# A 2-D Fourier mixing block on one core: the spectrum laid out image by image, the first transform in twelve groups of wider products

## The chip, the cores and the metric

The kernel runs on one NeuronCore of a Trainium2 chip. The metric is the device time of one execution in microseconds (us). The engines have their own instruction streams and meet by semaphores: TensorE (PE in the profile, its weight loads PEld), VectorE (DVE), ScalarE (ACT), GpSimd (POOL) and SyncE (SP), which only issues transfers here.

## What is computed

The input x is 4 images of 64 x 64 pixels with 16 channels, all float32. Two residual blocks follow each other. The change lies in the first half of the first one:

```python
h  = layernorm(x) @ w_te + b_te                  # 16 -> 32 channels
F  = fft2(h, axes=(1, 2))                        # over y and x
fr = concatenate([real(F), imag(F)])             # 64 channels
fc = gelu(fr @ w_fc + b_fc)                      # first channel mix, 64 -> 64
re, im = fc[..., :32], fc[..., 32:]
sp = real(ifft2(re + 1j * im))
x1 = x + sp @ w_tp + b_tp                        # second channel mix, 32 -> 16
h2 = layernorm(x1) @ w_fe + b_fe
x2 = x1 + gelu(depthwise3x3(h2) + b_dw) @ w_fp + b_fp
```

The second block (a 3x3 convolution to 192 channels, products of 8 x 8 Fourier patches, a layernorm, a gate and a projection) follows; the change leaves it alone.

## The kernel before, in words

Since the transform is linear, the kernel transforms the 16 normalised channels and not the 32 widened ones; `w_te` is folded into the weights of the first mix (`wmix1`), and the second mix (`wmix2`, 32 -> 16 channels) is done in the frequency domain too. Of the 64 frequencies u along y only U = 33 are computed.

**Load.** SP issues x in three pieces (group 0 in two halves, then group 1), `weights`, `more`, `w_qkv` and `norm2`; ScalarE issues `first` (tile `kf`, L600) and `taps`. A group g is two images; a plane is [128 rows (2 images x 64 y), 64 x] per channel. VectorE centres and normalises (L825 to L841), ScalarE squares and takes deviations (L612, L617); the result goes by channel into `sq` (`planes(g)`).

**First transform** (over y, TensorE, L1091 to L1106). Eight groups j of four channels; for each channel two products with the plane as the stationary operand, and `f1c` (cosines) or `f1s` (minus sines) as the moving one, 66 columns each (2 images x 33 u). They write partitions 0 to 63 and 64 to 127 of a PSUM bank. VectorE evacuates the even groups (L875), ScalarE the odd ones (L652 and L672), both by `f1_evac` (L325) into `f1`, which lies in the tile `spec`, channels innermost, so that the copy writes with a stride of 64 floats. `conv_weights` (L1076, which folds `w_qkv` for the second block and waits for its transfer) stands between groups 3 and 4. Five banks are used, so groups 5 to 7 wait for copies of earlier ones.

**Second transform** (over x, L1119 to L1130). For each u two products of 64 columns, with `dre` and `dim`, whose stationary operand is `f1[:, u]` (4 images x 16 channels = 64 columns). They give the real part on partitions 0 to 63 and the imaginary part on 64 to 127, rows ordered (part, image, channel). VectorE copies the banks into `sp` (L881), in five spans of 512 (the last of 64) frequencies.

**First mix** (`mix1`, L1156). For each span and each of the four images 64 output features are wanted twice over (128 columns, two sign patterns `s`), from the image's 16 real and 16 imaginary channels. These lie in different halves of the partitions. So a product takes 32 rows (the real or imaginary channels of two images, of which `wmix1` zeroes those of the other image), and each image takes two products that accumulate in one bank: a round of four (`again` false), a semaphore wait (`m1_half`), and a second round of four. The order of images is `QUADS`, the banks are `MIX_BANKS`. ScalarE applies Gelu to each bank (L685) into `gl`, which holds two spans.

**Second mix and column turn.** `mix2` (L1146) multiplies with `wmix2`, VectorE copies the result into `hc` (L886); `ht_step` (L1132) turns eight u with 64-column products, VectorE copies to `ht` (L889, L891). The order on TensorE, written out by hand at L1172 to L1183, is for span n: mix1(n), mix2(n-1), ht_step(n-2). Then comes the inverse transform (L1193, L1203).

**Beside it.** `wmix1` is made by ScalarE in eight copies (L664 to L667) from the product of `w_te` and `w_fc` in bank 7 (L1067), scaled by `smix` (GpSimd, L538); `hb` carries the bias to frequency zero (L669, L671; `mix_bias`, L1109). Behind group 7 ScalarE copies the folded conv weights (L676, L677) and loads the Gelu table; SP waits for that copy to issue eight loads of `wc` and eight of `wc9` (L448, L451), then the row of ones (L454, which waits for the last mix2); GpSimd waits for it to split the weights (L553 to L556) and then adds `b_tp` to x (L563).

## Time and profile before

| | us |
|---|---|
| runs (3) | 228.74, 226.67, 226.41; median 226.67 |
| profiled execution | 227.11 |
| its span, first to last instruction | 225.3 |
| TensorE busy in the span | 208.6 (93%) |
| VectorE, ScalarE, GpSimd busy | 156.2, 129.4, 77.2 |
| mean granted clock of TensorE | 0.997 of full speed |

Times in the rows are counted from the start of the span. A timeline row is: start, length, engine, line, operation, output and input tile, shapes, how many instructions are merged, and in brackets how long the engine had been idle and who released it. A row of a group is: line, engine, operation, tiles, shapes, count, then busy us, mean ns of one, then idle time before. A float32 matmul of the kernel appears as two instructions, so a count x8 is four products. Matmuls overlap; the length of a single one (some 220 ns for 64 columns) is mostly latency, and a merged row or a piece of the chain tells the rate. "DMA a<-b" is a transfer.

### The profile page before, as it was taken

The page shows a single profiled execution, that of the slowest core. Times are in us where ns is not written, and L with a number is a line of the kernel's source. Part 1 is how long each engine was busy: PE and PEld are TensorE (multiplying, and loading weights), DVE is VectorE, ACT ScalarE, POOL GpSimd, SP SyncE. Part 2 cuts the span into 40 slices and gives each one's busy share as a digit, 9 for nine tenths or more (in the row PEclk, how much of TensorE's full clock was granted, in tenths as well). Part 3 has the DMA queues.
Part 4 walks back from the last instruction along what each step waited for, and adds up shares of the span by engine and source line. Part 5 has one row for each costly group of instructions (what it writes and reads, how often), then busy time and mean ns, then how long its engine had stood idle before and what let it go on. Part 6 is the DMA issues. An engine that isn't in the chain of part 4 may idle for free.

```text
span 225.3 us, 4554 instructions
## 1 busy us (share of the span) xinstructions
PE 208.6 (93%) x1742; PEld 130.2 (58%) x1742; DVE 156.2 (69%) x286; ACT 129.4 (57%) x271; POOL 77.2 (34%) x70
## 2 busy tenths in 40 slices
PE   7969999898799999988899999999999999999973
PEld 3349624666357547864657565666657575665461
DVE  3995313539963991957886777897768986697693
ACT  3358176514384762754856767566665757565532
POOL 1553700000340000000166544663456435667800
PEclk9999999999999999999999999999999999999998
DMA  6940000000000039699999799999100000000002
GB/s 214 326 100 8 17 11 0 22 3 3 4 0 0 0 121 227 165 189 180 206 193 246 188 211 206 217 215 225 51 0 23 3 23 1 3 0 23 1 3 70
DMA packets 26006, 20.83 MB, mean 92 GB/s; under 512 B 5130, under 2 KB 24602, under 8 KB 25882
## 3 DMA queue, kind: packets, MB, share of 16 engines
q1 hardware_dynamic: 25355, 20.04, 42.4%
q10 hardware_dynamic: 629, 0.50, 0.8%
q8 instruction: 14, 0.23, 0.5%
q14 instruction: 8, 0.07, 0.1%
HBM read 16.36 MB, written 4.02 MB: 90 GB/s over the span
## 4 chain that ended last, share of the span: by engine, by line
PE 65%; DVE 14%; DMA 10%; ACT 4%; issue 3%; SPq 1%; ACTq 1%; DVEq 0%
PE psum L1293 22%; PE psum L1306 11%; PE psum L1325 6%; DMA wq<-w_qkv 5%; PE psum L1164 5%; PE psum L1237 4%; DMA parts<-tr 3%; PE psum L1343 2%; PE psum L1142 2%; PE psum L1152 2%; PE psum L1125 2%; PE psum L1369 2%; DVE tr L850 2%; DMA arena<-parts 2%; PE psum L1245 2%
## 5 line engine op out<-in xcount | busy, mean ns | idle before, releaser
L1293 PEld LDWEIGHTS psum<-wc,tile 128*128 128x128 f32 (+1 forms) x376 | 50.7, 160 | 25.7 <-issue 15.5
L1293 PE MATMUL psum<-wc,tile 128*128 128x192 f32 (+1 forms) x376 | 59.8, 309 | 3.1 <-DVE tile L386 1.4
L581 POOL TENSOR_TENSOR zp<-zp,ln 128x512 f32<-128x512 f32 x14 | 17.9, 1278 | 84.4 <-DVE zp L996 84.4
L1237 PE MATMUL psum<-arena,wdw 102*128 102x512 f32 x48 | 22.2, 597 | 1.3 <-ACT arena L341 1.3
L765 ACT ACTIVATE zp<-zp 128x512 f32<-128x512 f32 x15 | 9.5, 630 | 18.0 <-DVE zp L985 18.0
L969 DVE TENSOR_TENSOR arena<-psum,arena 128x1024 f32<-128x1024 f32 x15 | 18.3, 1219 | 1.8 <-ACT arena L754 1.8
L979 DVE TENSOR_REDUCE stat<-psum 128x8 f32<-128x512 f32 x16 | 11.0, 690 | 11.9 <-PE psum L1325 10.7
L582 POOL TENSOR_TENSOR zp<-zp,ln 128x512 f32<-128x512 f32 x14 | 18.2, 1298 | 1.1
L386 DVE COPY tile<-arena 128x256 f32<-128x256 f32 x64 | 15.3, 298 | 2.6 <-DMA arena<-parts 1.8
L612 ACT ACTIVATE sq<-xc 128x512 f32<-128x512 f32 x12 | 7.6, 637 | 16.4 <-DVE xc L829 16.4
L990 DVE TENSOR_REDUCE stat<-zp 128x8 f32<-128x512 f32 x15 | 10.3, 686 | 9.7 <-ACT zp L765 9.7
L386 ACT COPY tile<-arena 128x128 f32<-128x128 f32 x60 | 15.9, 318 | 1.4 <-DMA arena<-parts 1.4
L747 ACT COPY spec<-psum 128x768 f32<-128x768 f32 x16 | 12.6, 789 | 7.2 <-PE psum L1293 7.2
L1325 PE MATMUL psum<-arena,km 128*64 128x512 f32 x60 | 16.2, 617 | 0.4 <-DVE tr L855 0.4
L1306 PE MATMUL psum<-spec,km 64*128 64x512 f32 x64 | 15.9, 615 | 0.0
L685 ACT ACTIVATE arena<-psum,wt 128x512 f32<-128x512 f32 (+1 forms) x20 | 10.6, 612 | 9.0 <-PE psum L1164 9.0
L754 ACT COPY arena<-psum 128x1024 f32<-128x1024 f32 x15 | 14.9, 995 | 0.3 <-PE psum L1306 0.3
L1237 PEld LDWEIGHTS psum<-arena,wdw 102*128 102x128 f32 x48 | 8.5, 189 | 10.0 <-issue 8.6
L985 DVE SCALAR_TENSOR_TENSOR zp<-stat,psum 128x512 f32<-128x512 f32 x16 | 11.0, 688 | 1.8 <-DVE stat L979 0.5
L741 ACT COPY arena<-psum 128x512 f32<-128x512 f32 x16 | 9.5, 591 | 4.4 <-PE psum L1357 3.5
L886 DVE COPY spec<-psum 128x512 f32<-128x512 f32 (+1 forms) x5 | 3.0, 597 | 12.6 <-PE psum L1152 12.6
L996 DVE TENSOR_TENSOR zp<-zp,stat 128x512 f32<-128x512 f32 x16 | 11.1, 692 | 0.5
(138 smaller groups left out, 362.5 us busy)
## 6 DMA issues: line engine op xcount, KB each, us to landing
arena<-padded SPq DMA_DIRECT2D x12, 393.0 KB, 9.3
arena<-parts SPq DMA_DIRECT2D x12, 196.5 KB, 8.9
arena<-padded SPq DMA_DIRECT2D x6, 262.0 KB, 9.3
arena<-padded SPq DMA_DIRECT2D x8, 195.0 KB, 4.3
wq<-w_qkv SPq DMA_DIRECT2D x1, 1296.0 KB, 12.3
padded<-tr SPq DMA_DIRECT2D x4, 264.0 KB, 2.6
parts<-tr SPq DMA_DIRECT2D x9, 115.5 KB
out<-xt SPq DMA_DIRECT2D x8, 128.0 KB, 1.7
```

The lines of the kernel that those rows point to most:

```text
L386: o = copy(dst[:, n % 2, 2 * h:2 * h + 2].rearrange("p a (q x y) -> p (a q) x y", q=2, x=8), a)
L581: pool_link(pool.tensor_tensor(y, y, along(0), ALU.mult))
L582: pool_link(pool.tensor_tensor(y, y, along(1), ALU.add))
L747: act.copy(qkv[n // 2 % 4][:, n % 2].rearrange("p (a t) c -> p a (t c)", a=2), psum[:, 512 * conv_base(n):512 * conv_base(n) + 1024].rearr ...
L754: act.copy(kh, psum[:, 2048:3072]).then_inc(k_ev, 1)
L969: dve.tensor_tensor(pr, psum[:, 1024:2048], kh, ALU.mult).then_inc(prod, 1)
L996: dve.tensor_tensor(y, y, per_group(s[:, 3, :]), ALU.mult).then_inc(signal, 1)
L1164: last = mm(mix_bank(n, turn)[:, 0:w], wmix1[rows, b].rearrange("p s n -> p (s n)"), sp[rows, spans(n)], start=(n > 0 and not again), stop ...
L1237: last = mm(bank[4 + t4][:, :], wdw[:, dy].rearrange("p x h -> p (x h)"), uw[0:KW, 4 * t4:4 * t4 + 4, 2 * g:2 * g + 2, dy:dy + S], start=( ...
L1293: last = mm(bank[conv_base(n) + a][:, HID * h:HID * h + HID], stationary[:, n % 2, 2 * h + a, :], moving, start=first and h == 0, stop=not ...
L1306: last = mm(bank[2 + 2 * part + q][:, :], const(name)[rows], src, start=True, stop=True)
L1325: last = mm(o_bank(i)[64 * q:64 * q + 64, :], const("inv4"), pr[:, 512 * q:512 * q + 512], start=True, stop=True)
```

## The change

The moving matrices of the first transform become `f1a` and `f1b`, which each give real and imaginary part of the y transform, 132 columns. `f1a` (partitions 0 to 63) gives (cos, -sin), `f1b` (64 to 127) gives (-sin, -cos). `f1` becomes twice as large, [u, image, part, channel], and moves into the arena; the copy writes with a stride of 128 floats. A bank holds three channels of 132 columns, so there are twelve groups (four of three and two of two channels per pair of images), five for VectorE and seven for ScalarE. The second transform now uses `dre` alone and takes one image pair per product; the rows of `sp` come out as (image, part, channel), so an image's 32 values are one block of 32 partitions. `mix1` is then one round of four 32-row products, without accumulation and without `m1_half`; `wmix1` needs two copies instead of eight. On ScalarE the copies of the first transform now all stand behind `wmix1` and `hb`; on TensorE conv_weights stands between groups 5 and 6, behind group 5's wait for the copy of group 0.

```diff
-FIRST, NFIRST = columns(("f1c", 2 * U), ("f1s", 2 * U), ("mask", 2 * NB), ("sign", 1))
-MORE, NMORE = columns(("dre", S), ("dim", S), ("selre", S), ...
+FIRST, NFIRST = columns(("f1a", 4 * U), ("f1b", 4 * U), ("mask", 2), ("sign", 1))
+MORE, NMORE = columns(("dre", S), ("selre", S), ...
...
-QUADS = (0, 2, 1, 3)
 MIX_BANKS = (7, 3, 4, 0, 1, 5, 6, 7, 3, 4, 0, 1, 5, 7, 3, 4, 0, 1, 5, 7)
+F1_GROUPS = [(g, slice(c, min(c + n, C))) for g in range(G2) for c, n in ((0, 3), (3, 3), (6, 3), (9, 3), (12, 2), (14, 2))]
+F1_VECTOR, F1_SCALAR = (4, 5, 6, 8, 10), (0, 1, 2, 3, 7, 9, 11)
...
-    put("f1c", np.einsum("ab,yu->aybu", eye2, np.cos(th)).reshape(P, 2 * U))
-    put("f1s", np.einsum("ab,yu->aybu", eye2, -np.sin(th)).reshape(P, 2 * U))
+    put("f1a", np.einsum("ab,ryu->aybru", eye2, [np.cos(th), -np.sin(th)]).reshape(P, 4 * U))
+    put("f1b", np.einsum("ab,ryu->aybru", eye2, [-np.sin(th), -np.cos(th)]).reshape(P, 4 * U))
...
-        f1 = spec[:, 0:UV].rearrange("p (u b c) -> p u b c", u=U, b=NB)
+        f1 = arena[:, 12416:12416 + 2 * UV].rearrange("p (u b r c) -> p u b r c", u=U, b=NB, r=2)
...
-        wmix1 = sb("wmix1", [P, NB, 2, 2 * H0])
+        wmix1 = sb("wmix1", [P, 2, 2 * H0])
...
-            return bank[(0, 1, 2, 3, 4, 0, 1, 2)[j]]
+            return bank[j % 5 if j < 6 else (j - 5) % 5]
...
-            src = f1_bank(j)[:, 0:4 * 2 * U].rearrange("p (c b u) -> p c b u", c=4, b=2)
-            return copy(f1[:, :, 2 * g:2 * g + 2, 4 * c4:4 * c4 + 4].rearrange("p u b c -> p c b u"), src)
+            src = f1_bank(j)[:, 0:4 * U * n].rearrange("p (c b u) -> p c b u", c=n, b=4)
+            return copy(f1[:, :, 2 * g:2 * g + 2, :, cs].rearrange("p u b r c -> p c (b r) u"), src)
...
             square(0, 0)
             deviation(0, 0)
-            square(0, 1)
-            deviation(0, 1)
-            for j in (1, 3):
-                act.wait_ge(f1_mm, j + 1)
-                f1_evac(act.copy, j).then_inc(f1_act, 1)
-
             act.wait_ge(ld_w, 16)
...
             act.activation(wmix2[:, :], const("tp"), ACT.Copy, scale=const("sign")).then_inc(mix_ready, 1)
+            square(0, 1)
+            deviation(0, 1)
...
-            for b in range(NB):
-                for s in range(2):
-                    act.activation(wmix1[:, b, s, :], bank[7][:, 0:2 * H0], ACT.Copy,
-                                   scale=smix[:, NB * s + b:NB * s + b + 1]).then_inc(mix_ready, 1)
-
+            for s in range(2):
+                act.activation(wmix1[:, s, :], bank[7][:, 0:2 * H0], ACT.Copy, scale=smix[:, s:s + 1]).then_inc(mix_ready, 1)
             act.activation(hb[:, 0:1], bank[7][0:H0, 64:65], ACT.Identity, bias=vec("b_te", H0)).then_inc(act_chain, 1)
-            act.wait_ge(act_chain, 1)
-            act.activation(hb[:, 1:2], hb[:, 0:1], ACT.Copy, scale=float(S * S)).then_inc(mix_ready, 1)
-            for j in (5, 7):
+            for j in F1_SCALAR:
                 act.wait_ge(f1_mm, j + 1)
                 f1_evac(act.copy, j).then_inc(f1_act, 1)
+                if j == 0:
+                    act.wait_ge(act_chain, 1)
+                    act.activation(hb[:, 1:2], hb[:, 0:1], ACT.Copy, scale=float(S * S)).then_inc(mix_ready, 1)
...
-            for j in range(0, 8, 2):
+            for j in F1_VECTOR:
                 dve.wait_ge(f1_mm, j + 1)
                 f1_evac(dve.tensor_copy, j).then_inc(f1_dve, 1)
...
-            for r in range(2):
-                mm(bank[7][64 * r:64 * r + 64, 0:2 * H0], const("teT", H0), fc[:, r, :], start=True, stop=True)
+            te_T = const("teT", H0)
+            for b in range(NB):
+                for r in range(2):
+                    mm(bank[7][H0 * b:H0 * b + H0, 0:2 * H0], te_T[:, H0 * r:H0 * r + H0], fc[:, r, :], start=(r == 0), stop=(r == 1))
...
-            for j in range(8):
-                g, c4 = divmod(j, 4)
-                if j == 4:
+            for j, (g, cs) in enumerate(F1_GROUPS):
+                if j == 5:
+                    pe.wait_ge(f1_act, 1)
+                if j == 6:
                     conv_weights()
-                if j == 5:
-                    pe.wait_ge(f1_dve, 1)
-                if j == 6:
-                    pe.wait_ge(f1_act, 1)
-                if j == 7:
-                    pe.wait_ge(f1_dve, 2)
+                    pe.wait_ge(f1_act, 2)
+                if j in (7, 8):
+                    pe.wait_ge(f1_act, j - 4)
+                if j >= 9:
+                    pe.wait_ge(f1_dve, j - 8)
                 pe.wait_ge(z_done, half_no(0, g, 1))
-                for c in range(4):
-                    for r, name in enumerate(("f1c", "f1s")):
-                        last = mm(f1_bank(j)[64 * r:64 * r + 64, 2 * U * c:2 * U * (c + 1)], planes(g)[:, 4 * c4 + c, :], const(name),
-                                  start=True, stop=True)
+                for c in range(cs.start, cs.stop):
+                    for r, name in enumerate(("f1a", "f1b")):
+                        at = 4 * U * (c - cs.start)
+                        last = mm(f1_bank(j)[64 * r:64 * r + 64, at:at + 4 * U], planes(g)[:, c, :], const(name), start=True, stop=True)
                 last.then_inc(f1_mm, 1)
...
-            pe.wait_ge(f1_act, 2)
-            pe.wait_ge(f1_dve, 3)
-            for turn in range(3):
-                mix_bias(turn)
+            mix_bias(0)
+            pe.wait_ge(f1_dve, 4)
+            mix_bias(1)
+            pe.wait_ge(f1_act, 6)
+            mix_bias(2)
             pe.wait_ge(ld_more, 16)
-            pe.wait_ge(f1_act, 4)
-            pe.wait_ge(f1_dve, 4)
+            pe.wait_ge(f1_act, 7)
+            pe.wait_ge(f1_dve, 5)
...
                 for u in range(8 * n, min(8 * n + 8, U)):
-                    for r, name in enumerate(("dre", "dim")):
-                        last = mm(f2_bank(n)[64 * r:64 * r + 64, S * (u % 8):S * (u % 8) + S],
-                                  f1[:, u].rearrange("p b c -> p (b c)"), const(name), start=True, stop=True)
+                    for g in range(G2):
+                        last = mm(f2_bank(n)[64 * g:64 * g + 64, S * (u % 8):S * (u % 8) + S],
+                                  f1[:, u, 2 * g:2 * g + 2].rearrange("p b r c -> p (b r c)"), const("dre"), start=True, stop=True)
...
-                for turn, b in enumerate(QUADS):
-                    r = turn // 2 if not again else 1 - turn // 2
-                    rows = slice(64 * r + 32 * (b // 2), 64 * r + 32 * (b // 2) + 32)
-                    at = NB * n + turn
-                    if MIX_BANKS[at] in MIX_BANKS[:at] and not again:
+                for b in range(NB):
+                    rows = slice(H0 * b, H0 * b + H0)
+                    at = NB * n + b
+                    if MIX_BANKS[at] in MIX_BANKS[:at]:
                         pe.wait_ge(gelu1, max(i for i in range(at) if MIX_BANKS[i] == MIX_BANKS[at]) + 1)
-                    last = mm(mix_bank(n, turn)[:, 0:w], wmix1[rows, b].rearrange("p s n -> p (s n)"), sp[rows, spans(n)],
-                              start=(n > 0 and not again), stop=again, skip_group_check=(n == 0))
-                    if again:
-                        last.then_inc(m1_mm, 1)
-                if not again:
-                    last.then_inc(m1_half, 1)
+                    mm(mix_bank(n, b)[:, 0:w], wmix1[rows].rearrange("p s n -> p (s n)"), sp[rows, spans(n)],
+                       start=(n > 0), stop=True, skip_group_check=(n == 0)).then_inc(m1_mm, 1)
...
                 pe.wait_ge(f2_ev, 5 if n == 1 else n + 1)
-                mix1(n, False)
-                pe.wait_ge(m1_half, n + 1)
-                mix1(n, True)
+                mix1(n)
```

## Rows read from the trace of the kernel before

**Rows 1.** page of the profile: granted clock in 40 slices, chain by engine

```profile
PEclk9999999999999999999999999999999999999998
...
PE 65%; DVE 14%; DMA 10%; ACT 4%; issue 3%; SPq 1%; ACTq 1%; DVEq 0%
```

**Rows 2.** chain of waits, first 48 us: start, us, what

```profile
3.07 12.32 DMA wq<-w_qkv
...
15.44 1.52 PE psum L1081 x16
...
17.57 2.02 PE psum L1104 x64
...
20.34 3.94 PE psum L1125 x128
...
24.86 1.11 PE psum L1164 x8
...
26.01 3.03 PE psum L1164 x16
...
45.23 2.72 PE psum L1193 x118
```

**Rows 3.** timeline, 10 to 20 us: start, us, engine, line, operation

```profile
12.02 2.09 PE L1104 MATMUL psum<-kf,sq 128*64 128x66 f32 x64 [0.95 <-DVE sq L841]
...
14.53 0.32 ACT L617 ACTIVATE st<-st,eps 128x32 f32<-128x32 f32 x1 [0.47 <-DVE st L835]
...
16.33 1.66 ACT L666 ACTIVATE wmix<-psum,smix 128x64 f32<-128x64 f32 x8
...
17.50 1.95 PEld L1104 LDWEIGHTS psum<-kf,sq 128*64 128x64 f32 x64 [0.30 <-DVE sq L841]
...
17.89 0.24 ACT L669 ACTIVATE hb<-psum,wt 32x1 f32<-32x1 f32 x1
...
19.63 0.60 ACT L325 COPY spec<-psum 128x264 f32<-128x264 f32 x1 [0.32 <-PE psum L1104]
```

**Rows 4.** groups of instructions by line and shape, 0 to 60 us

```profile
L841 DVE TENSOR_TENSOR sq<-xc,st 128x512 f32<-128x512 f32 x4 | 4.3, 1068 | 0.1
...
L881 DVE COPY arena<-psum 128x512 f32<-128x512 f32 x4 | 2.8, 692 | 2.5 <-PE psum L1125 2.5
...
L325 ACT COPY spec<-psum 128x264 f32<-128x264 f32 x4 | 2.3, 628 | 0.6 <-PE psum L1104 0.6
L325 DVE COPY spec<-psum 128x264 f32<-128x264 f32 x4 | 2.3, 614 | 0.5 <-PE psum L1104 0.3
...
L677 ACT COPY x<-psum 128x384 f32<-128x384 f32 x1 | 0.5, 457 | 0.0
```

**Rows 5.** DMA issues, 0 to 20 us

```profile
kf<-first ACTq DMA_DIRECT2D x1, 70.5 KB, 3.3
```

**Rows 6.** timeline, 27 to 43 us, the channel mixes

```profile
27.17 2.42 ACT L685 ACTIVATE arena<-psum,wt 128x512 f32<-128x512 f32 x4 [4.91 <-PE psum L1164]
27.91 0.29 PEld L1164 LDWEIGHTS psum<-arena,wmix 32*128 32x128 f32 x2 [0.73 <-ACT arena L685]
...
30.16 1.07 PE L1152 MATMUL psum<-arena,wmix 128*32 128x512 f32 x8
...
31.16 2.37 PE L1164 MATMUL psum<-arena,wmix 32*128 32x512 f32 x16
...
34.45 1.15 PE L1142 MATMUL psum<-km,spec 128*64 128x64 f32 x32
...
39.91 0.99 PE L1164 MATMUL psum<-arena,wmix 32*128 32x64 f32 x16
...
42.90 0.32 PE L1152 MATMUL psum<-arena,wmix 128*32 128x64 f32 x8
```

**Rows 7.** timeline, work issued behind the copies of the conv weights

```profile
22.39 4.40 POOL L563 TENSOR_TENSOR xt<-xt,wt 128x512 f32<-128x512 f32 x4
...
26.32 6.03 SPq L451 DMA_DIRECT2D wc<-w9s  x8
```

More of the change, by code:

```diff
@@ L85, in constants @@
     put("dre", np.concatenate([co, si]))
-    put("dim", np.concatenate([-si, co]))
-    mask = np.zeros((2, NB, C, 2, NB))
-    for b in range(NB):
-        mask[:, b, :, 0, b] = 1
-        mask[0, b, :, 1, b] = 1
-        mask[1, b, :, 1, b] = -1
-    put("mask", mask.reshape(P, 2 * NB))
+    mask = np.ones((NB, 2, C, 2))
+    mask[:, 1, :, 1] = -1
+    put("mask", mask.reshape(P, 2))
     sign = np.ones((P, 1))
@@ L149, in put @@
         w[row:row + a.shape[0], lo:lo + a.shape[1]] = a
-    for b in range(NB):
-        put("teT", i["L0_conv_w_te"].T, at=C * b)
+    for r in range(2):
+        put("teT", i["L0_conv_w_te"].T, at=3 * C * r)
     put("te", i["L0_conv_w_te"])
@@ L236, in two_blocks @@
         ui9_pairs = arena[:, 3 * UW:4 * UW].rearrange("p (i x t y) -> p i x t y", i=2, x=8, t=8)
-        smix = sb("smix", [P, 2 * NB])
-        wmix1 = sb("wmix1", [P, NB, 2, 2 * H0])
+        smix = sb("smix", [P, 2])
+        wmix1 = sb("wmix1", [P, 2, 2 * H0])
         hb = sb("hb", [H0, 2])
@@ L680, in _ @@
                 w = spans(n).stop - spans(n).start
-                for turn, b in enumerate(QUADS):
-                    act.wait_ge(m1_mm, NB * n + turn + 1)
+                for b in range(NB):
+                    act.wait_ge(m1_mm, NB * n + b + 1)
                     if n >= 2:
                         act.wait_ge(m2_mm, n - 1)
-                    act.activation(gl[:, n % 2, b, 0:w], mix_bank(n, turn)[:, 0:w], ACT.Gelu, bias=vec("b_fc")).then_inc(gelu1, 1)
+                    act.activation(gl[:, n % 2, b, 0:w], mix_bank(n, b)[:, 0:w], ACT.Gelu, bias=vec("b_fc")).then_inc(gelu1, 1)
             load_table(ACT.Sqrt)
@@ L1153, in mix2, with mix1 @@
                 last.then_inc(m2_mm, 1)
-            def mix1(n, again):
+            def mix1(n):
                 w = spans(n).stop - spans(n).start
-                for turn, b in enumerate(QUADS):
-                    r = turn // 2 if not again else 1 - turn // 2
-                    rows = slice(64 * r + 32 * (b // 2), 64 * r + 32 * (b // 2) + 32)
-                    at = NB * n + turn
-                    if MIX_BANKS[at] in MIX_BANKS[:at] and not again:
-                        pe.wait_ge(gelu1, max(i for i in range(at) if MIX_BANKS[i] == MIX_BANKS[at]) + 1)
-                    last = mm(mix_bank(n, turn)[:, 0:w], wmix1[rows, b].rearrange("p s n -> p (s n)"), sp[rows, spans(n)],
-                              start=(n > 0 and not again), stop=again, skip_group_check=(n == 0))
-                    if again:
-                        last.then_inc(m1_mm, 1)
-                if not again:
-                    last.then_inc(m1_half, 1)
+                for b in range(NB):
+                    rows = slice(H0 * b, H0 * b + H0)
+                    at = NB * n + b
+                    if MIX_BANKS[at] in MIX_BANKS[:at]:
+                        pe.wait_ge(gelu1, max(i for i in range(at) if MIX_BANKS[i] == MIX_BANKS[at]) + 1)
+                    mm(mix_bank(n, b)[:, 0:w], wmix1[rows].rearrange("p s n -> p (s n)"), sp[rows, spans(n)],
+                       start=(n > 0), stop=True, skip_group_check=(n == 0)).then_inc(m1_mm, 1)
             pe.wait_ge(m1_bias, NB)
```

15 lines of the change are left out of this document (8 added, 7 removed).

## The prediction

> **What bounds the kernel now.** I read the page first: the chain that ended last is 65% TensorE and 14% VectorE, and the granted clock is at its upper level (2.4 GHz) in all but the last of 40 slices [rows 1]. So in the stage that the change touches, the question is what TensorE does or waits for. The chain of waits in order of time answers it [rows 2]: the `w_qkv` transfer lands at 15.40; conv weights (L1081, L1084) run 15.44 to 17.57; the second group's first transform 2.02 us; then an evacuation and the mix bias until 20.34; the second transform to 24.86; then the two channel mixes and the column turn (`ht_step`) until the inverse transform starts at 45.23. From 15.4 to 45.2 this is TensorE nearly throughout. The timeline shows who works beside it [rows 3, 6], the groups by shape give prices [rows 4].
>
> All times below are of the profiled execution: 227.11 us, which is a span of 225.3 and 1.8 around it. It lies 0.44 above the median 226.67 of the three runs; I take that off at the end.
>
> **Part 1, the mix: one round instead of two.** Start to start, L1152 at 30.16, L1164 at 31.16 and L1142 at 34.45 [rows 6]: 3.29 from the start of two rounds of mix1 to that of the column turn, of which mix2 takes 1.00 (30.16 to 31.16), so the two rounds take 2.29, and one with its gap 1.15; the first round of all has 1.11 and then 0.04 until the next at 26.01 [rows 2]. The short span's two rounds take 0.99 with their tail [rows 6], say 0.49 each. The change drops four of the long and one of the short: 4 x 1.18 is at most 4.7, plus 0.45: about 5.1 us of TensorE.
>
> Not all of it reaches the end, because ScalarE's Gelu takes 2.42 us for a span of four [rows 6], more than the 1.15 of a round. I walk the stage, with mix1(0) starting at t = 0, a product ready 1.15 after its round starts (26.01 to 27.17), a Gelu 0.605 (2.42 / 4), mix2 1.00 and ht 1.08 (1.15 with its tail, less the 0.07 by which mix2's 1.07 exceeds 1.00), and 0.06 for a semaphore:
> - Gelu span 0: 1.15 to 3.57. mix1(1) starts at 1.11, but its fourth product needs bank 7, as now (TensorE waits 0.73 for that Gelu [rows 6]); it starts at 1.89 and ends at 3.0.
> - Gelu 1: 3.57 to 5.99. mix2(0) must wait for Gelu 0: 3.63 to 4.67, after an idle 0.6. mix1(2) to 5.78. Gelu 2: 5.99 to 8.41.
> - mix2(1) waits for Gelu 1: 6.05 to 7.09 (idle 0.27). ht(0) to 8.17, mix1(3) to 9.28; Gelu 3: 9.32 to 11.74.
> - mix2(2) to 10.28, ht(1) to 11.36, mix1(4) to 11.81, mix2(3) to 12.85, ht(2) to 13.93, mix2(4) to 14.18, ht(3) to 15.29; two VectorE copies and a semaphore, as now, and L1193 starts at 16.2.
>
> Now it is 45.23 - 24.86 = 20.37. So 4.2 us are gained, and 0.9 of the 5.1 goes into waits for Gelu. The Trainium skill warns of just this (TensorEngine Tiling (Array Packing), PSUM Bottleneck): once tiling has made TensorE faster, the evacuation of PSUM may be the limit. If Gelus alone set the stage, the last would end about 1.0 earlier than in my walk, so the rule gives no worse time; here it takes 0.9 of the gain.
>
> **Part 2, the first transform: twice the columns.** Per channel there are still two products (four instructions), in two column groups that overlap. Now: 2.02 / 16 = 126 ns a channel with 66 columns [rows 2]. What do 66 more cost? L1152 with 64 and with 512 columns takes 0.32 and 1.07 us for two instructions per column group [rows 6]: 0.75 / (2 x 448) = 0.84 ns per column and instruction, so 2 x 66 x 0.84 = 110 ns. A channel becomes 236 ns, 16 of them 3.78 us instead of 2.02. Bounds: 220 ns (nothing but columns) and 252 (twice 126), 3.52 and 4.03 us. Gaining below 220 is the first rival. I take 236, from the row of the same kind of instruction.
>
> The Trainium skill (TensorEngine Tiling (Array Packing), Instruction Overhead) gives each matmul some 60 cycles beside its columns. By that a channel would rise by (132 + 60) / (66 + 60), to 192 ns; no row here has 132 columns.
>
> **Part 3, who evacuates and in what order.** `f1` doubles, so copies are of 396 or 264 elements. Strided 264 cost VectorE 0.61, strided 512 (L841) about 1.05 [rows 4]: 1.7 ns an element, so 396 cost 0.84. ScalarE: 264 cost 0.605 [rows 3, 4]; with 0.2 fixed, 396 cost 0.81. Bounds for ScalarE: 0.46, the plain copy of 384 (L677), and 1.21, two of today's. I take 0.81, nearest to the row with the same kind of write. The stride between written elements doubles (256 to 512 bytes); VectorE's plain and strided rows (0.69 and 1.07 for 512) tell only that striding costs, not how it grows.
>
> ScalarE no longer copies at 14.75 but first makes `wmix1` (2 instead of 8) and `hb`: the deviations end at 14.85 [rows 3], 2 at 1.66 / 8 and hb 0.24 bring it to 15.48, the copy of group 0 ends at 16.29. Only then may TensorE begin group 5 (bank 0 again), and conv_weights stands behind group 5:
> - Group 5 (2 channels): 16.35 to 16.82. Conv weights, 17.57 - 15.44 = 2.13 [rows 2], to 18.95. Today they started with the landing; this moved wait costs 1.4.
> - Second group: 18.95 + 3.78 = 22.73. Its bank waits are covered: ScalarE's copies 1, 2, 3 end at 17.3, 18.1 and 18.9 (with hb's 0.2 between), TensorE needs them at 18.95, 19.7 and 20.4; VectorE is free after the normalise that released 17.50 [rows 3] and copies 4 and 5 by 18.5, group 6 by 20.6, needed at 22.3.
> - Group 11: copied 22.77 to 23.38, against 19.63 to 20.23 [rows 3]. The mix bias fits beside it. The second transform starts at 23.46 instead of 20.34: 3.12 us later. Its work is unchanged (same instructions, same 64 columns).
> The weight copies of ScalarE (L676, L677) come 3.1 later, and behind them SP's loads of `wc` and POOL's additions: these ended at 32.35 and 26.79 [rows 7], now at 35.5 and 29.9; both are needed only behind the inverse transform that starts at 44 [rows 2], so this costs nothing. SP's next load, the row of ones, waits behind them for mix2(4), at about 42: 6 us are left; without that cover the depthwise stage would wait for it. The Gelu table is loaded in time too.
>
> **Part 4, the loads.** `first` grows by 126 columns (63 KB), `more` shrinks by 64 (32 KB). `kf` is issued together with the first half of x and took 3.3 us for 70.5 KB [rows 5]; in that stretch the kernel's queues share the engines. The start at 3.85 may move by 0 to 0.2; everything in part 3 hangs on it, so I take 0.1. The eight tiny products for `wmix1` run where TensorE idles 0.95 before 12.02 [rows 3]: nothing.
>
> **Sum.** +3.12 + 0.1 - 4.17 (20.37 - 16.2) = -0.95, and the inverse transform starts at 44.3. From there the chain is bound to the shifted work, so I pass all of it on: 227.11 - 0.95 = 226.16, and on the scale of the median 225.7 us.
>
> **Rivals.**
> - A, wider products are cheaper than I say. Weight loads are busy 1.95 of the 2.09 us of a 16-channel stretch [rows 3], so these and not the columns may set 126 ns today. If a channel cost 192, the second group is 0.70 and group 5 0.09 shorter: 224.9 (on the median's scale). Against: the 0.84 ns per column, which makes 220 from columns alone. This is what the skill's 60 cycles would give.
> - B, slower than before: ScalarE's copies set the pace. At 1.5 us for 396 elements, group 0 is out at 16.98, group 5 and the conv weights end at 19.6, and copies 1, 2, 3, 7, 9 run back to back: 18.7, 20.2, 21.7, 23.2, 24.7; then group 11's 1.0: the second transform starts at 25.8, 5.4 later instead of 3.1: 228.0. It decides above about 1.2 us a copy: there the copies are back to back and the gain of 4.2 is used up (transform at 24.3, +4.0, and 0.1 of part 4). For: 1.21 is today's price per element without any fixed part, and the stride doubles. Against: VectorE's rows show a fixed part.
> - C, the gain is not passed on: a later stage with its own pace (a DMA, 10% of the chain [rows 1]) absorbs the 0.95: 226.7. For: such transfers stand in the chain. Against: behind the mixes they are loads of what the kernel itself has just stored, so they shift too.
> - D, the clock falls in the new idle of 1.1 us before group 5. At half the clock, conv weights, second group and half of the second transform take 8 us longer: 234. Against: today TensorE idles 1.33 us just there (14.11 to 15.44) and the clock stays up [rows 1 to 3].
>
> **Chances.** Forecast 0.62; A 0.12; B 0.10; C 0.12; D 0.02; other 0.02. A measurement tells from no change about 1%, 2.3 us. Faster by over that needs A beyond its price together with cheap copies: 0.07. Slower by over 1% needs B beyond 1.7 us a copy, or D: 0.05. Range: cheapest bounds together (columns 220, copies of 0.46, no delay of x: 0.3, 0.55 and 0.1 less) give 224.8, A 224.9, B 228.0; with the spread of the runs I give 224.5 to 227.6.
>
> **What would show it.** The stretch of 32 instructions per column group with 132 columns takes 3.8 us; ScalarE's 396-element copy 0.81, VectorE's 0.84; conv weights start at 16.8; the second transform at about 23.5; mix1 no longer runs in rounds, TensorE waits 0.6 and 0.3 for Gelu before mix2(0) and mix2(1); L1193's counterpart starts at 44.3. I am wrong if the second transform starts before 22.5 or after 24.5, if the mix stage isn't 16.2 long, or if the lead at 44 isn't in the total.

## The result and the profile after

The changed kernel takes 224.88 us in the median of 20 runs, the kernel before 226.97 (20 runs): 2.1 less by the medians. The ratio leaves out slow executions, those over 1.5% above the fastest of the same kernel (one of each kernel's 20), and is 0.9925 with a 95% interval of 0.990 to 0.995, so 1.7 us (1.1 to 2.3) less. The forecast was 0.95 less. The difference is under 1%, so it falls into the forecast's middle class, and 224.88 lies in its range (224.5 to 227.6), yet the gain is larger than forecast by more than the interval allows.

One thing has to be said about the profile shown here: in that execution (228.36 us, span 226.6) TensorE's granted clock fell near 100 us. Up to 95 us it is like the others. The first experiment below is the same kernel again, and its profile (span 222.7) has the clock up all along.

**The first 44 us.** The timeline of the changed kernel, answering to [rows 3] and [rows 6]: start, us, engine, line, operation.

```profile
12.19 3.37 PE L1099 MATMUL psum<-kf,sq 128*64 128x132 f32 x56 [0.35 <-DVE sq L833]
...
14.92 0.50 ACT L659 ACTIVATE wmix<-psum,smix 128x64 f32<-128x64 f32 x2
...
15.46 0.81 ACT L323 COPY arena<-psum 128x396 f32<-128x396 f32 x1
...
16.17 2.28 ACT L323 COPY arena<-psum 128x396 f32<-128x396 f32 x3
...
16.32 0.67 PE L1099 MATMUL psum<-kf,sq 128*64 128x132 f32 x8 [0.76 <-ACT arena L323]
...
16.92 1.52 PE L1075 MATMUL psum<-wq,wt 96*32 96x384 f32 x16
...
18.98 3.82 PE L1099 MATMUL psum<-kf,sq 128*64 128x132 f32 x64
19.93 0.85 DVE L323 COPY arena<-psum 128x396 f32<-128x396 f32 x1 [1.68 <-PE psum L1099]
...
23.55 3.95 PE L1120 MATMUL psum<-km,arena 128*64 128x64 f32 x128
...
28.00 3.02 PE L1158 MATMUL psum<-arena,wmix 32*128 32x512 f32 x16
...
29.16 7.05 ACT L677 ACTIVATE arena<-psum,wt 128x512 f32<-128x512 f32 x12 [3.67 <-PE psum L1158]
...
31.64 1.06 PE L1147 MATMUL psum<-arena,wmix 128*32 128x512 f32 x8 [0.61 <-ACT arena L677]
...
33.95 1.06 PE L1147 MATMUL psum<-arena,wmix 128*32 128x512 f32 x8 [0.18 <-ACT arena L677]
```

Read it downward. L1099 is the first transform. Five groups, 14 channels, take 3.37 us; then TensorE stands idle for 0.76 until ScalarE's copy of group 0 (15.46, 0.81 us) lets group 5 begin at 16.32, and the conv weights (L1075) stand behind it at 16.92, where they began at 15.44 before. The second group takes 3.82 us from 18.98, and the second transform starts at 23.55. The mix then runs in single rounds: mix1(0) and mix1(1) are merged into 3.02 us from 28.00, and ScalarE does twelve Gelus without a break from 29.16 (7.05 us), where in the kernel before they came in fours of 2.42 us [rows 6] with idle times of 0.66 and 0.88 between the first three fours.

The chain of waits of the same stage, answering to [rows 2]: start, us, what.

```profile
28.07 1.11 PE psum L1158 x8
29.18 3.60 ACT arena L677 x7
...
33.17 0.74 ACT arena L677
33.91 0.04 issue
33.95 1.06 PE psum L1147 x8
35.02 1.08 PE psum L1137 x32
36.10 1.07 PE psum L1158 x8
...
44.07 2.72 PE psum L1181 x120
```

For 4.3 us (3.60 and 0.74) the chain is ScalarE's Gelu (L677), which it never was in this stage before; then TensorE takes over, mix2 (L1147), the column turn (L1137) and one round of mix1 (L1158, 1.07) in turn. The inverse transform starts at 44.07 instead of 45.23.

**Behind it.** Windows of the changed kernel: us, busy time of PE, PEld, DVE, ACT, POOL, granted clock, DMA share, GB/s.

```profile
96.00:98.00 2.00, 0.00 (x0) 0.00 (x0) 0.49 (x3) 0.49 (x3) 0.00 (x0) 1.00 0.94 220
98.00:100.00 2.00, 1.86 (x9) 1.72 (x10) 1.93 (x6) 1.17 (x4) 0.00 (x0) 0.78 1.06 196
100.00:102.00 2.00, 2.00 (x9) 1.17 (x9) 0.39 (x2) 0.80 (x1) 0.00 (x0) 0.50 1.26 189
102.00:104.00 2.00, 2.00 (x11) 0.73 (x10) 0.20 (x1) 1.01 (x1) 0.00 (x0) 0.87 1.26 202
```

TensorE does nothing from 96 to 98, and the granted clock is 0.78, 0.50 and 0.87 in the three windows behind, where 0.50 is its lower level, 1.2 GHz. Its timeline shows the same: the second convolution group's last products at 94.09, the third group at 98.14, and its 12 instructions take 2.60 us instead of 1.87:

```profile
94.09 1.56 PE L1281 MATMUL psum<-w,zp 16*128 16x192 f32 x8
98.14 2.60 PE L1281 MATMUL psum<-wc,tile 128*128 128x192 f32 x12 [2.48 <-DVE tile L384]
100.66 2.89 PE L1294 MATMUL psum<-spec,km 64*128 64x512 f32 x8
```

The chain of waits tells what the third group waits for. Kernel before:

```profile
87.56 5.66 DMA parts<-tr
...
94.11 3.76 DMA arena<-parts
...
98.51 1.87 PE psum L1293 x12
```

Changed kernel, run again (first experiment):

```profile
86.25 5.12 DMA parts<-tr
...
92.37 2.93 DMA arena<-parts
...
95.95 1.87 PE psum L1281 x12
97.82 1.08 PE psum L1294 x4
```

Both times these are two transfers in a row, the store of the split rows (`parts<-tr`) and the load of them (`arena<-parts`). Here they take 5.12 and 2.93 us, there 5.66 and 3.76. So the third group starts at 95.95 instead of 98.51, a lead of 2.56 us, of which only 1.3 stem from the start of the inverse transform (43.93 against 45.23). The rest is not a property of the changed kernel alone: in its first profile, the one with the fallen clock, the same two take 5.46 and 4.79, and the third group starts at 98.14.

What releases the third group in the two kernels is VectorE's copy of the loaded rows into `tile`. Kernel before:

```profile
97.89 0.49 DVE L386 COPY tile<-arena 128x256 f32<-128x256 f32 x2 [1.82 <-DMA arena<-parts]
98.51 1.87 PE L1293 MATMUL psum<-wc,tile 128*128 128x192 f32 x12 [1.03 <-DVE tile L386]
```

Changed kernel, run again:

```profile
95.33 0.50 DVE L384 COPY tile<-arena 128x256 f32<-128x256 f32 x2 [1.42 <-DMA arena<-parts]
95.95 1.87 PE L1281 MATMUL psum<-wc,tile 128*128 128x192 f32 x12 [0.41 <-DVE tile L384]
```

TensorE has been idle for 1.03 and 0.41 us there. So without an extra product the third group waits for these rows, and an earlier end of the first and second group only makes the idle longer.

The landmarks of all profiles but e3's in one table, in us from the start of the span; "turn" is TensorE's first channel turn (L1254 before, `channel_major(0)`), "first" and "third" the first instructions of conv(0) and conv(2), "tail" the rest of the span from there. The clock is the mean granted clock. The rows of e1 to e12 are explained with their experiments; e3, which starts the inverse transform at 48.58 and the first convolution group at 97.54 with its clock down, is told there.

| profile | inverse transform | turn | first | first - turn | third | tail | clock |
|---|---|---|---|---|---|---|---|
| before | 45.23 | 78.10 | 91.46 | 13.36 | 98.51 | 126.8 | 0.997 |
| changed | 44.07 | 76.92 | 89.68 | 12.76 | 98.14 | 128.5 | 0.990 |
| e1, changed again | 43.93 | 76.82 | 89.57 | 12.75 | 95.95 | 126.8 | 1.000 |
| e2, conv weights first | 43.17 | 76.03 | 88.78 | 12.75 | 96.73 | 128.5 | 0.989 |
| e4, changed + 2 products | 44.09 | 76.99 | 89.75 | 12.76 | 97.75 | 126.8 | 0.997 |
| e5, changed + 1 product | 44.03 | 76.91 | 89.66 | 12.75 | 96.71 | 126.8 | 0.996 |
| e9, the same again | 44.22 | 77.10 | 89.85 | 12.75 | 96.72 | 126.7 | 0.998 |
| e6, before + 1 product | 44.92 | 77.77 | 91.17 | 13.40 | 98.31 | 126.8 | 1.000 |
| e10, the same again | 45.09 | 77.97 | 91.41 | 13.44 | 98.45 | 126.8 | 0.996 |
| e7, e2 + 1 product | 43.29 | 76.16 | 89.02 | 12.86 | 97.17 | 126.7 | 0.997 |
| e8, e7 + `first` later | 42.99 | 75.87 | 88.62 | 12.75 | 95.49 | 126.7 | 1.000 |
| e11, e5 + 0.5 us delay | 44.84 | 77.72 | 90.48 | 12.76 | 97.34 | 126.7 | 0.996 |
| e12, e5 + 1 us delay | 45.13 | 78.01 | 90.77 | 12.76 | 98.98 | 128.4 | 0.989 |

The tail is 126.7 to 126.8 in every profile of the table but the three whose clock fell, where it is 1.7 longer. The whole time is thus settled when the third group starts, up to that 1.7.

### The profile page after: what moved, and what is told of

Read it like the earlier page. It is cut to its first block, busy times and chain, and to the rows that moved or that the text cites. A ratio compares the mean times of both kernels' runs of the same rounds, so it can differ in the third digit from the quotient of the medians.

```text
span 226.6 us, 4499 instructions
## 1 busy us (share of the span) xinstructions
PE 209.6 (93%) x1714; PEld 132.9 (59%) x1714; DVE 157.3 (69%) x287; ACT 131.2 (58%) x268; POOL 77.2 (34%) x70
## 4 chain that ended last, share of the span: by engine, by line
PE 62%; DVE 18%; ACT 8%; DMA 6%; issue 3%; ACTq 1%; SPq 0%; DVEq 0%
PE psum L1281 22%; PE psum L1294 12%; PE psum L1313 6%; PE psum L1225 4%; DMA parts<-tr 2%; DVE xc L821 2%; PE psum L1331 2%; DMA arena<-parts 2%; DVE st L817 2%; PE psum L1099 2%; PE psum L1137 2%; ACT arena L677 2%; PE psum L1120 2%; PE psum L1357 2%; DVE tr L842 2%
## 5 line engine op out<-in xcount | busy, mean ns | idle before, releaser
L1281 PE MATMUL psum<-wc,tile 128*128 128x192 f32 (+1 forms) x376 | 60.5, 311 | 4.1 <-DVE tile L384 2.9
L1294 PE MATMUL psum<-spec,km 64*128 64x512 f32 x64 | 16.8, 645 | 0.0
L1313 PE MATMUL psum<-arena,km 128*64 128x512 f32 x60 | 16.2, 617 | 0.4 <-DVE tr L847 0.4
L677 ACT ACTIVATE arena<-psum,wt 128x512 f32<-128x512 f32 (+1 forms) x20 | 10.5, 619 | 4.7 <-PE psum L1158 4.6
L1050 PE MATMUL psum<-arena 128*128 128x512 f32 x16 | 10.2, 794 | 1.4 <-POOL arena L531 1.4
```

Of the source, the lines that this page charges most:

```text
L677: act.activation(gl[:, n % 2, b, 0:w], mix_bank(n, b)[:, 0:w], ACT.Gelu, bias=vec("b_fc")).then_inc(gelu1, 1)
L1281: last = mm(bank[conv_base(n) + a][:, HID * h:HID * h + HID], stationary[:, n % 2, 2 * h + a, :], moving, start=first and h == 0, stop=not ...
L1294: last = mm(bank[2 + 2 * part + q][:, :], const(name)[rows], src, start=True, stop=True)
L1313: last = mm(o_bank(i)[64 * q:64 * q + 64, :], const("inv4"), pr[:, 512 * q:512 * q + 512], start=True, stop=True)
```

## The experiments

Each run below also lists how many of its executions had a mean granted clock under 0.995 ("fallen"); such executions took about 2 us longer, and the others are called undisturbed. For the changed kernel it was 6 of the 20 runs (median 226.7, the other 14: 224.8). The kernel before was run again beside each set of experiments: 29 times beside e1 to e4 (median 226.29, 4 fallen), 29 beside e5 to e8 (227.79, 14 fallen), 35 beside e9 to e12 (226.30, 3 fallen). The ratios are to these.

**e1: the changed kernel again.** No edit.

> The changed kernel itself, on the same chip as the three below. Theory (the stage gives 1.2 us at 44 us of the span and it is passed on): 1.2 to 1.5 us faster than before, the inverse transform's first products at 44.1, the next convolution stage 1.2 us earlier than before all along, where the clock stays up. Rival (the lead is lost at the transfers that land near 98 us, and what is measured comes from something else): the third convolution group starts at 98 as in the profile of before, with the lead gone there.

Measured: ratio to before 0.9962 (0.9923 to 1.0001), median 227.16 of 12, but 7 of 12 fallen (median 227.95); the five others took 224.5 to 226.2, median 225.35, where before had 226.28 (25 of 29). The inverse transform starts at 43.93. So in the executions with the clock up the lead is there and 0.9 us of it are passed on (225.35 against 226.28), less than the 1.2 to 1.5 expected; the rival, that it is gone by 98 us, falls in them. In the profile in which it was gone, the transfers had landed late. Over all its executions the changed kernel was no faster here: its clock fell in 7 of 12, that of the kernel before in 4 of 29. What had to be explained now was the clock, and the spread of the third group's start.

**e2: conv_weights before group 5.**

```diff
                 if j == 5:
+                    conv_weights()
                     pe.wait_ge(f1_act, 1)
                 if j == 6:
-                    conv_weights()
                     pe.wait_ge(f1_act, 2)
```

> conv_weights before group 5 instead of behind it. Theory (the moved wait costs time: TensorE idles until group 0 is copied, 15.5 to 16.3, with the conv weights queued behind): conv weights start at 15.5, the second transform at 22.6 instead of 23.55, the inverse transform at 43.1, the whole 0.9 us faster than the change. Rival (VectorE's normalise or ScalarE's copies set the second group's pace anyway): second transform at 23.3 or later, total the same within 0.3.

TensorE's timeline of e2:

```profile
12.28 3.37 PE L1099 MATMUL psum<-kf,sq 128*64 128x132 f32 x56 [1.28 <-DVE sq L833]
15.58 1.52 PE L1075 MATMUL psum<-wq,wt 96*32 96x384 f32 x16
...
17.64 4.27 PE L1099 MATMUL psum<-kf,sq 128*64 128x132 f32 x72
...
22.66 1.56 PE L1120 MATMUL psum<-km,arena 128*64 128x64 f32 x46
```

The conv weights start at 15.58 and the second transform at 22.66, 0.9 earlier than in the changed kernel, although x landed 0.1 later; the inverse transform starts at 43.17. The order of these two waits is worth what the theory said, up to there. The total isn't: ratio to before 0.9985 (0.9953 to 1.0017), with 10 of 12 executions fallen. The two others took 224.65 and 225.42. The idle before the third group is 2 us in its profile, and part of the lead had gone into more of that.

**e3: each round of the first mix twice**, with the semaphore between them.

```diff
+                    last = mm(mix_bank(n, b)[:, 0:w], ...)
+                last.then_inc(m1_half, 1)
+                pe.wait_ge(m1_half, n + 1)
+                for b in range(NB):
+                    rows = slice(H0 * b, H0 * b + H0)
                     mm(mix_bank(n, b)[:, 0:w], ...).then_inc(m1_mm, 1)
```

> Each round of the first mix is done twice, with the semaphore wait between the two as before the change (span 0 is thereby added twice). Theory (the rounds are what the change saves, less the waits for Gelu): mix1(0) to the inverse transform takes 20.3 us instead of 16.0, the whole 4.3 us slower than the change and 3 slower than before. Rival (ScalarE's Gelu bounds the stage, so a round is mostly hidden): less than 2.5 us slower than the change.

The chain of waits of e3 (L1159 and L1165 are the two rounds):

```profile
28.20 1.11 PE psum L1159 x8
...
29.36 1.14 PE psum L1165 x8
30.50 1.89 PE psum L1159 x8
...
48.58 2.71 PE psum L1188 x124
```

From mix1(0) at 28.20 to the inverse transform at 48.58 it is 20.38 us, the 20.37 of the kernel before almost to the last digit [rows 2], against 16.0 in the changed kernel (28.07 to 44.07). So the second rounds are worth 4.4 us, not the 5.1 of TensorE's time in it: the rest would be Gelu's waits. The fastest of the six executions took 230.13 (median 232.54), 5.6 above e1's fastest and 4.2 above that of before, so about 1 us more than the start of the inverse transform explains (48.58 against 43.93 and 45.23). The profile is of another, the slowest (236.27, mean clock 0.974): in it the load of the tap rows, which e10 and e12 come to, took 6.5 us, longer than anywhere else, TensorE stood idle for 3.19 before the first convolution group, and the granted clock was 0.50 from 96 to 106. So a delay as large as this one seems to cost more than itself. The ratio to before is 1.021 (1.016 to 1.027). The rival (under 2.5 us) falls.

**e4: two products of 512 columns before the third convolution group**, so that TensorE isn't idle there.

```diff
                 conv(2 * s + 1)
+                if s == 0:
+                    keep_warm(2, km, 3)
```

> Two products of 512 columns into a free bank, 1.7 us of TensorE, between the second and the third convolution group, where the profile of the changed kernel shows TensorE idle for 2.5 us before 98.1 and the granted clock at its lower level from 98.4 to 103.7. Theory (the idle there lets the clock fall in a part of the executions, at 1.7 to 2 us each): no execution with a mean granted clock of 0.99 is left, the median is unchanged or up to 0.3 lower, the spread smaller. Rival (the clock falls whatever TensorE does there): the share of executions at 0.99 stays near 5 of 20, and the median rises by up to 0.3 where the products delay the convolution.

None of 12 executions fell, and they lie within 225.89 to 226.65. Against 7 of 12 in e1 on the same chip: with the idle filled the clock stayed up. But the median is 226.09, 0.7 above e1's undisturbed runs (225.35) and 1.3 above those of the first 20 (224.8): two products take until about 97.6, and the third group starts at 97.75 where it started at 95.95 in e1. In this profile its data came no sooner either (VectorE's copy at 97.12, and the group starts 0.6 behind that copy as in e1), but no execution of the twelve came below 225.89, while e1's fastest took 224.53. The expectation had put that cost at 0.3 at most.

**e5: one such product** (`keep_warm(1, km, 3)`).

> The changed kernel with one product of 512 columns (0.96 us) between the second and the third convolution group, instead of two. Theory (two took away the fall of the clock but delayed the third group to 97.6 where its data can be there at 95.8): few or no executions at a clock of 0.99, third group at 96.7 or when its transfer lands, median 225.0 to 225.5, below that of before by 1 us. Rival (one product does not keep the clock up): a third or more of the executions at 0.99, 2 us longer than the rest.

```profile
95.57 1.12 PE L1050 MATMUL psum<-km 128*128 128x512 f32 x2
96.71 1.54 PE L1281 MATMUL psum<-wc,tile 128*128 128x192 f32 x8
```

The product (L1050) ends and the third group follows at once, at 96.71. (Its data were there no sooner: VectorE's copy starts at 96.07.) 1 of 12 fell; median 225.10, eleven of them within 225.0 to 226.13; ratio to before 0.9912 (0.9874 to 0.9950), 1.96 below the undisturbed runs of the kernel before on that chip (15 of 29, median 227.06).

**e6: the kernel before with the same product.**

> The kernel before the change with the same one product. Theory (the fall of the clock is a property of the idle time before the third group and not of the change): its executions at 0.99 go too, its median stays at 226.1 to 226.4, so that e5 against this one shows the change alone: 1.1 to 1.3 us by the lead at the inverse transform. Rival (the change gains more or less than its lead behind 44 us): e5 and this one differ by under 0.6 or over 1.8.

0 of 12 fell, where 14 of 29 of the plain kernel before did on the same chip. Median 227.02: not 226.1 to 226.4, so e5 against e6 is 1.92, above the 1.8 of the rival. The leads in the table are 0.9 at the inverse transform, 1.5 at the first convolution group, 1.6 at the third. Something behind the change's own stage goes faster too, in the kernels with a product.

**e7: e2 and one product together.**

> conv_weights before group 5 and the one product together. Theory (conv_weights first leads by 0.8 to 0.9 at the inverse transform; its median was spoilt by the fallen clock in 10 of 12 executions): 0.8 us faster than e5, median 224.2 to 224.7, faster than both kernels. Rival (the third group waits for transfers that do not move with the lead): the same as e5 within 0.3.

Six executions, none fallen, 224.13 to 225.74, median 225.18: the same as e5 (ratio to before 0.9897, 0.9841 to 0.9954). The inverse transform starts 0.74 earlier than in e5, but the third group at 97.17 waits 1.07 for its data (`tile` copied by VectorE from `arena<-parts`). In its profile x landed at 4.24, the latest of all. So the rival holds in this profile: what the lead gives, the landing takes.

**e8: e7, and `first` issued by SyncE behind x.**

```diff
 # SyncE
             sp_.dma_start(xt[:, 1], xin[1]).then_inc(ld_x1, 16)
+            sp_.dma_start(kf[:, :], first).then_inc(ld_first, 16)
 # ScalarE
-            act.dma_start(kf[:, :], first).then_inc(ld_first, 16)
```

> As e7, and the constants of the first transform are issued by SyncE behind the three pieces of x instead of by ScalarE beside the first. Theory (kf, twice as large, shares the engines with the first half of x, which landed at 3.88 to 4.12 in the changed kernels): VectorE starts at 3.7 to 3.85, everything up to the inverse transform 0.2 earlier than in e7, total 0.2 faster. Rival (the landing of x varies by itself): start between 3.85 and 4.1 as before, total the same.

VectorE's first instruction in e8:

```profile
3.44 0.69 DVE L817 TENSOR_REDUCE st<-xt 128x32 f32<-128x512 f32 x1 [3.44 <-DMA xt<-x]
```

It starts at 3.44, 0.4 to 0.8 earlier than in any other profile (3.84 to 3.88 in the three of the kernel before, 3.88 to 4.24 in the ones with `first` twice as large). Of the 0.8 against e7 0.3 are kept: the inverse transform starts at 42.99 and 43.29. 0 of 12 fell, 223.99 to 225.87, median 224.91; ratio to before 0.9887 (0.9853 to 0.9922). It has the fastest single execution of all (e5's best is 225.00, e7's 224.13), but its median is only 0.2 below e5's and 0.3 below e7's, well inside the intervals, so that the whole is faster is not shown.

**e9 to e12: is the lead passed on one for one?** e9 is e5 again, e10 is e6 again, on one chip with two kernels that start the inverse transform later by a product in a free bank:

```diff
             pe.wait_ge(ht_ev, 5)
+            keep_warm(1, km, 6, 512)     # e12; 256 columns in e11
```

> The kernel of e5 again, as the base of the three below on one chip. Median 225.1; the third convolution group at 96.7; from TensorE's channel turn (76.9) to the first convolution group 12.75.

> The kernel of e6 again. Theory (the lead of the change grows from 0.9 to 1.5 between the channel turn and the first convolution group, by a habit of this stage and not by chance): 1.7 to 2.0 slower than e9, from the channel turn to the first convolution group 13.4 as in both profiles of the kernel before. Rival (the 13.4 was chance of the transfers' landing): 12.75 in this profile and 1.0 to 1.3 slower than e9.

> The kernel of e9 with one product of 256 columns into a free bank ahead of the inverse transform: it starts 0.45 to 0.5 later, nothing else changes. Theory (behind 44 us a delay is passed on one for one): 0.5 slower than e9. Rival (a delay there costs more than itself, because it changes what the transfers of the tap rows and of the parts meet): 0.8 or more.

> The same with 512 columns, 0.9 to 1.0 later: the inverse transform starts where it does in the kernel before. Theory of one for one: 1.0 slower than e9, and then 0.9 faster than e10, which has the same start, so that what is left lies in the kernel before and not in the time of the start. Rival: 1.7 to 2.0 slower than e9 and the same as e10, with 13.4 from the channel turn to the first group: the start time alone decides.

By the medians a delay cost nothing (e9 226.41 and 3 of 12 fallen, e11 226.45 and 2, e12 226.39 and 2), and e10 (227.53 and 3) is 1.1 above e9. But the medians are blurred, because the executions with the clock up fall into clusters too: e11 has six at 225.66 to 225.83 and four at 227.08 to 227.31. Taking it that a late landing only adds, I compare the early clusters, which are narrow but chosen after the fact: e9 225.10 to 225.21 (three), e11 225.66 to 225.83 (six), e12 226.03 to 226.31 (six), e10 227.03 to 227.16 (five). By the profiles the inverse transform starts 0.6 (e11) and 0.9 (e12) later than in e9, and the clusters lie 0.5 to 0.6 and 0.9 to 1.1 higher. In the profiles the third group of e11 starts 0.62 later than that of e9, as the inverse transform does. So one for one holds for these two delays as far as the early clusters tell, and the rival falls with them; the medians can't confirm it. Of the expectations, e9's median of 225.1 was missed; e10's 1.7 to 2.0 above e9 holds between the early clusters (1.9) and not between the medians, and its 13.4 from the turn to the first group holds (13.44).

The kernel before without a product took 226.30 in the same set, with 3 of 35 fallen: e9's ratio to it is 0.9983 (0.9947 to 1.0018), e11's 1.0000, e12's 1.0004, and e10's 1.0053 (1.0021 to 1.0085). So here the product cost the kernel before more than it gave back, and the changed kernel with it was no faster than the kernel before without it.

But e12 and e10 start the inverse transform together (45.13 and 45.09) and are 0.9 apart in these clusters. The table tells where: from the turn to the first convolution group e12 takes 12.76 and e10 13.44. The timelines of that stretch, e10 (kernel before with one product):

```profile
84.73 0.45 SPq L493 DMA_DIRECT2D zp<-padded  x1
...
88.08 2.82 PE L1245 MATMUL psum<-wt,arena 128*128 128x96 f32 x24
...
90.43 1.35 ACT L392 COPY zp<-zp 16x256 f32<-16x256 f32 x4 [1.29 <-DMA zp<-padded]
...
91.41 0.89 PE L1293 MATMUL psum<-wc,tile 128*128 128x192 f32 x4 [0.52 <-ACT zp L392]
```

and e12:

```profile
84.79 0.45 SPq L491 DMA_DIRECT2D zp<-padded  x1
...
88.11 2.81 PE L1234 MATMUL psum<-wt,arena 128*128 128x96 f32 x24
...
89.36 1.35 ACT L390 COPY zp<-zp 16x256 f32<-16x256 f32 x4 [0.15 <-DMA zp<-padded]
...
90.77 1.49 PE L1282 MATMUL psum<-wc,tile 128*128 128x192 f32 x8
```

Everything up to the projection (88.08 and 88.11) is equal within 0.06. SyncE issues the load of the tap rows (`zp<-padded`, 65 KB) at 84.73 and 84.79. In e10 it lands so that ScalarE gathers at 90.43, in e12 at 89.36, and the first convolution group needs it. From issue to landing it is 5.7 us in e10 and 4.6 in e12.

The three profiles of the kernel before have 5.6, 5.0 and 5.7 us for this transfer (in the one with 5.0, e6, a Gelu behind ScalarE's slow store issues, 5.26 us instead of 4.4, held the projection before the group instead), the ten of the changed family in the table 4.3 to 5.1, e3's, with its later start, 6.5. In the profiles with a product this reaches the third group, since TensorE works without a break up to it (all but e7 and e12, which wait there 1.07 and 1.19 us for its data). Why the load takes longer in the kernel before I don't know. The code of the two around that transfer is the same; what differs is where tensors lie, and how large `first`, `more` and `wmix1` are. It wasn't tried to move them.

## Why the prediction was right, and what it missed

**Part 1, the mix: right.** The walk gave 16.2 us from mix1(0) to the inverse transform; it is 16.0. TensorE waits for Gelu before mix2(0) (0.6) and mix2(1) (0.18, I had 0.27), as walked, and e3 puts the second rounds at 4.4 us net. The Trainium skill's warning (TensorEngine Tiling (Array Packing), PSUM Bottleneck) is that evacuation may take over once tiling has made TensorE faster. The chain agrees, though here TensorE got faster by a round less and not by tiling: 4.3 us of ScalarE stand in it that weren't there.

**Part 2, the first transform: right.** Forecast 236 ns a channel; measured 3.75 / 16 = 234 in the chain of waits at 19.05. Rival A is dead with it. The Trainium skill (TensorEngine Tiling (Array Packing), Instruction Overhead) gives some 60 cycles of overhead for each matmul; the estimate made from that was 192. The measurement decides, and the slope of L1152's two rows was the better guide. The weight loads being busy nearly all the time was no sign that they bind: the same 64 were busy for 1.95 us before and for 3.57 now, so they stretch with the products.

**Part 3, the copies and the order: right.** A copy of 396 takes VectorE 0.85 us and ScalarE 0.87 by the mean of its six, 0.76 each where three stand back to back (2.28), against forecasts of 0.84 and 0.81, so rival B is dead. One of its reasons was a slip: 0.605 us for 264 elements without any fixed part makes 0.91 for 396, and not 1.21, which is the price of two copies. Conv weights at 16.92 instead of 15.44, second transform at 23.55 against the forecast 23.56. e2 shows the price of that order, 0.9 us at the second transform and not the 1.3 by which conv weights move (15.58 against 16.92), since group 5 then comes behind them.

**Part 4, the loads.** The term of 0.1 was at the low side: x lands at 3.88 to 4.24 where `first` is twice as large and issued beside it (ten profiles, mean 4.08), at 3.84 to 3.88 before (three, mean 3.86), so it costs 0.2. That x's landing hangs on `kf` is shown by e8, which issues `kf` later and brings 3.44.

**The sum: the term that was too small is the last, that the lead is passed on as it is.** Up to 44 us the forecast of 0.95 stands against 0.9 to 1.3 in the profiles. But I took the rest of the kernel to be the same in both, and between 77 and 98 us it is not. Where an extra product fills TensorE's idle, the tap rows and ScalarE's issues decide: the first convolution group gains another 0.6, and like starts still end 0.9 apart (e10, e12). The two plain kernels, which the forecast is about, don't take that path, since their third group waits for the split rows. From the channel turn to VectorE's copy of these it is 19.8 to 19.9 us in the three profiles of the kernel before (78.10 to 97.89 in the first) and 18.5 to 20.6 in the ten of the changed family (76.82 to 95.33 in e1, 76.92 to 97.51 in the first). So of the 1.7 measured about 1.2 is the change's own stage, the rest lies in when these transfers land, and why they land as they do is open. Part of it may be the luck of the set: with the clock up the difference was 0.9 in e1's.

Rival C, that a stage with its own pace absorbs the lead, is not what the result or the early clusters of e11 and e12 show. It is not dead for every execution: in the first profile of the changed kernel the third group starts only 0.37 earlier than before (98.14 against 98.51), and e9's median is that of the plain kernel before.

**Rival D looked at the wrong gap.** The clock doesn't fall in the 0.76 us before group 5. In the changed kernel it falls at the third convolution group, some 80 us behind that gap, and costs 1.7 us in the tail. In the kernel before it falls too, by the clocks of its executions, but no profile shows where; that it is the same place is argued from e6 (0 of 12 against 14 of 29), and e10 (3 of 12 against 3 of 35) doesn't bear it out. The lead itself may feed this: e1 and e2, which come to the wait earlier, had 7 and 10 of 12 fallen, the kernel before 4 of 29 on the same chip. I had read the clock as a row of nines of one execution. The before kernel's own runs had told it: 228.74 against 226.41 and 226.67.

## What to carry to other kernels

Price wider products by the slope between two rows of the same kind with different columns, and walk a stage of two engines instruction by instruction with such rows: that gave the start of each stage here to 0.2 us. Then look behind the stage as well: the next place where all wait for a transfer decides what a lead is worth, and if TensorE is idle there, whether its clock comes back whole; one dummy product there left 11 of 90 executions fallen (e5 to e12), where the changed kernel without it had 13 of 32, for some 0.3 us (e5's 225.10 against 224.8, the undisturbed runs without it); a second one left none of 12 and cost 1 us more. These are counts of different chips and sets, and in the last set 10 of 48 fell with a product and 3 of 35 of the kernel before without one, so measure it beside the plain kernel before it is kept. When a time is spread over clusters, compare like with like (clock and cluster) as well as the medians, and tell both: e1's median lies 0.9 above that of before though its undisturbed runs are 0.9 below.

## What the runs showed of the hardware

- TensorE's granted clock went to its lower level (1.2 GHz, 0.50 in the windows) behind idle times of 3.2 us (e3), 2.5 (changed kernel), 2.0 (e2) and 1.2 (e12), and stayed up behind 1.0 (before) and 1.1 (e7). In the changed kernel, e2 and e12 it cost 1.7 us in the tail. Twelve instructions of the third group took 2.60 us behind the fall and 1.87 without it.
- A 65 KB load took 4.3 to 5.1 us in one kernel and 5.0 to 5.7 in another; where it was issued within 0.06 us of the same time (e10 and e12), 5.7 and 4.6.
- A copy with a strided write costs per element the same at strides of 256 and of 512 bytes, on VectorE: 264 elements took 0.61 us at 256 bytes and 0.60 at 512, and 396 took 0.85 at 512.
- The same 64 weight loads were busy 1.95 us beside products of 66 columns and 3.57 beside products of 132, where 16 channels took 2.02 and 3.75.
- What is issued beside x moves its landing: it comes at 3.44 with `kf` issued behind x (e8), at 3.88 to 4.24 with `kf` beside it (ten profiles).
